# A graph kernel on one core: the edges' attention scores picked with one-hot products, in four parts, instead of gathered in two

## The reference

```python
h_proj = jnp.einsum('nd,rde->rne', h, relation_weight)
t_r = h_proj[etype, src]
h_r = h_proj[etype, dst]
att = jnp.sum(t_r * jnp.tanh(h_r + efeat), axis=-1)
seg_max = jax.lax.stop_gradient(jax.ops.segment_max(att, dst, num_segments=N))
att_exp = jnp.exp(att - seg_max[dst])
denom = jax.ops.segment_sum(att_exp, dst, num_segments=N)
a = att_exp / denom[dst]
h_nb = jax.ops.segment_sum(h[src] * a[:, None], dst, num_segments=N)
out = leaky_relu((h + h_nb) @ res_w1.T) + leaky_relu(h * h_nb @ res_w2.T)
```

## Time and profile before

| | us |
|---|---|
| median of three runs | 4488.78 |
| lowest and highest of them | 4483.08, 4492.01 |
| the profiled execution's own time | 4494.4 |
| its span | 4492.4 |
| busy: PE, DVE, ACT, POOL | 1605.1, 2361.7, 1340.0, 3099.8 |

### The profile page before, as it was taken

The page is one execution under the profiler, slowest core; times in us unless marked ns, Lnnn a source line. Parts: engine busy times, 40 slices in busy tenths (PEclk is TensorE's granted clock), DMA queues, the critical chain, the costliest instruction groups (busy, mean ns, idle before and its releaser), DMA issues.

```text
span 4492.4 us, 34467 instructions
## 1 busy us (share of the span) xinstructions
PE 1605.1 (36%) x8878; PEld 1252.6 (28%) x8878; DVE 2361.7 (53%) x3528; ACT 1340.0 (30%) x2772; POOL 3099.8 (69%) x3293
## 2 busy tenths in 40 slices
PE   6600088888566420000000000033356400466564
PEld 2200066666444210000000000022245300466553
DVE  9959877888899768887701111022222200444442
ACT  0012255656333211111110000122222100687773
POOL 8877787100388767777577777777747777487787
PEclk9955588999777655555555555555566555666665
DMA  2147777666344335555422222243433200122121
GB/s 52 40 131 247 239 225 235 219 211 225 117 123 120 95 111 196 175 200 186 170 58 73 74 73 74 89 127 124 129 95 92 82 1 0 35 58 62 56 57 28
DMA packets 362656, 528.19 MB, mean 118 GB/s; under 512 B 220064, under 2 KB 232458, under 8 KB 362470
## 3 DMA queue, kind: packets, MB, share of 16 engines
q1 hardware_dynamic: 268166, 426.25, 28.6%
q0 software_dynamic: 94304, 99.74, 9.5%
HBM read 265.55 MB, written 264.24 MB: 118 GB/s over the span
## 4 chain that ended last, share of the span: by engine, by line
POOL 53%; issue 18%; DVE 16%; PE 5%; DMA 4%; ACT 3%; SPq 1%; POOLq 0%; DVEq 0%; ACTq 0%
POOL arena L1202 21%; POOL result L1197 9%; POOL slot_rows L1197 8%; POOL relf L1202 8%; POOL work L1202 6%; DMA arena<-in_x 3%; DVE arena L522 1%; DVE arena L508 1%; POOL pause L1210 1%; DVE t_stat L513 1%; DVE t_stat L506 1%; PE banks L1611 1%; DVE arena L538 1%; DVE work L565 1%; DVE arena L561 1%
## 5 line engine op out<-in xcount | busy, mean ns | idle before, releaser
L1202 POOL DMA_INDIRECT arena<-input_and_place_by_node,src_i x252 | 313.2, 1243 | 461.0 <-DVE arena L641 386.5
L1197 POOL DMA_INDIRECT result<-work,outi x392 | 479.3, 1223 | 169.2 <-issue 122.1
L1202 POOL DMA_INDIRECT arena<-g_by_node_and_edge,m_idx x392 | 447.0, 1140 | 121.1 <-issue 119.2
L1202 POOL DMA_INDIRECT work<-in_x,dsafe x392 | 432.9, 1104 | 117.1 <-issue 62.3
L1197 POOL DMA_INDIRECT slot_rows<-work,dsafe x392 | 402.4, 1027 | 139.9 <-issue 119.2
L1202 POOL DMA_INDIRECT arena<-h_by_node_and_edge,m_idx x392 | 400.7, 1022 | 119.5 <-issue 119.2
L1202 POOL DMA_INDIRECT relf<-slot_scores,src_i x392 | 371.2, 947 | 150.1 <-issue 68.3
L1701 PE MATMUL banks<-ident,work 128*128 128x128 f32 x456 | 112.1, 395 | 874.3 <-DMA work<-slot_rows 873.2
L822 DVE TENSOR_TENSOR work<-work,ends 128x896 f32<-128x896 f32 x28 | 46.7, 1669 | 561.8 <-DMA work<-h_by_node_and_edge 556.5
L1701 PEld LDWEIGHTS banks<-ident,work 128*128 128x128 f32 x456 | 81.1, 204 | 890.2 <-issue 689.6
L565 DVE SCALAR_TENSOR_TENSOR work<-work 128x1024 f32<-128x1024 f32 (+1 forms) x77 | 116.6, 1514 | 298.3 <-ACT work L1520 238.9
(11 more groups left out here) (320 smaller groups left out, 5606.4 us busy)
## 6 DMA issues: line engine op xcount, KB each, us to landing
arena<-in_x SPq DMA_DIRECT2D x96, 512.0 KB, 5.2
slot_rows<-work SPq DMA_DIRECT2D x48, 912.0 KB, 8.7
work<-slot_rows SPq DMA_DIRECT2D x114, 384.0 KB, 3.3
input_and_place_by_node<-arena SPq DMA_DIRECT2D x49, 528.0 KB, 2.7
arena<-input_and_place_by_node SPq DMA_DIRECT2D x49, 512.0 KB
g_by_node_and_edge<-arena SPq DMA_DIRECT2D x49, 512.0 KB, 2.6
h_by_node_and_edge<-arena SPq DMA_DIRECT2D x49, 512.0 KB, 2.6
arena<-x_of_destination SPq DMA_DIRECT2D x56, 448.0 KB, 4.1
```

The costliest lines, as they stand in the source:

```text
L1197: pool.indirect_dma_start(out=table[:, :], out_offset=bass.IndirectOffsetOnAxis(ap=idx, axis=0), in_=of, in_offset=None, bounds_check=boun ...
L1202: pool.indirect_dma_start(out=to, out_offset=None, in_=table[:, :], in_offset=bass.IndirectOffsetOnAxis(ap=idx, axis=0)).then_inc(signal, 16)
```

## The change

Edges are split into four parts in the order in which they are sent: steps 0 to 7, 8 to 15, 16 to 23 and 24 to 27 of the permute stage, that is 112, 112, 112 and 56 columns. Each part has its own slots: 144, 144, 144 and 88 tiles, 520 in place of 456, so 130 quadruples in place of 114. Part 0 is counted in the first edge stage and placed in the second; parts 1 to 3 are counted and placed inside the permute stage (`sort_next`): 32 counts in step 0, 8 and 16, and 32 placements over the next five steps.

A score now stays in SBUF. An edge knows its tile and its lane. For a pair of columns TensorE spreads the edges' lanes over the partitions (`spread_lanes`), VectorE compares them with the partition's own number, which gives a one-hot matrix (`lanes_hot`), TensorE multiplies that with the part's scores, so that each edge's partition holds the scores of its lane in all tiles (`find_scores`), and VectorE picks the edge's tile with a compare, a multiply and a sum, one instruction a column (`scores_picked`). There are 196 pairs.

`spread_work` sets how many quadruples and pairs stand in each step, by a room of 35 a step, 3.0 a quadruple and 1.9 a pair. Its table, worked out from the code: steps 9, 10 and 11 have 11 quadruples of part 0 each, step 12 has 3 and 13 pairs, steps 13 and 14 have 18 pairs, step 15 has 7. Steps 17 to 23 repeat that with part 1. Steps 25, 26 and 27 have 11 quadruples of part 2 each. What is left stands after the last step: 3 quadruples and 56 pairs of part 2, then 22 quadruples and 28 pairs of part 3. The 392 gathers of scores and the two stores are gone. The four relation numbers come with one load. The slots' zeroing is 60 stores of 1664 columns in place of 48 of 1824.

```diff
-HALF = KE // 2
-KH = 228
-KS = 2 * KH
+PART_STEPS = (0, 8, 16, 24, 28)
...
+            runs, room = [[] for _ in range(GE + 1)], 0.0
+            left = [(k, kind, cost, n) for k in range(PARTS)
+                    for kind, cost, n in (("score", 3.0, PART_TILES[k] // RG), ("pick", 1.9, (PART_COLS[k][1] - PART_COLS[k][0]) // 2))]
...
+            def lanes_hot(i):
+
+                dve.wait_ge(pick["spread"], i + 1)
+                after(dve, pick["found"], i - 1)
+                ts(lane_hot[:, i % 2, :], bank(6)[:, 0:2 * P], lane_no[:, 0:1], None, ALU.is_equal).then_inc(pick["hot"], 1)
+
+            def scores_picked(k, i):
+
+                dve.wait_ge(pick["found"], i + 1)
+                n = PART_TILES[k]
+                for c in range(2):
+                    t = 2 * i_column(k, i) + c
+                    after(dve, pick["done"], 2 * i + c)
+                    stt(out=picked[:, 0:n], in0=tile_no[:, 0:n], scalar=tile_of[:, t:t + 1], in1=bank(7)[:, c * KH:c * KH + n],
+                        op0=ALU.is_equal, op1=ALU.mult, accum_out=att[:, t:t + 1]).then_inc(pick["done"], 1)
...
             step_c(0)
             for s in range(GE):
                 if s + 1 < GE:
                     step_c(s + 1)
-                rel_some(*first_part_span(s))
-            rel_some(NJ, 2 * NJ)
-
-
-            o = Steps(dve, soft)
-            dve.wait_ge(score_got, 16 * KE)
+                sort_next(s)
+                follow(s)
+            follow(GE)
+
+
+            o = oe
+            dve.wait_ge(pick["done"], KE)
...
-            pool.wait_ge(sort, at_step["score rows"])
-            for k, at in enumerate((range(HALF, KE), range(0, HALF))):
-                pool.wait_ge(scored, 16 * (k + 1))
-                for t in at:
-                    (gather if k else gather_slowly)(att[:, t:t + 1], att_t[k], score_row[:, t:t + 1], score_got)
...
-                number = [pe.value_load(tile_reli[0:1, j * RG + k:j * RG + k + 1], min_val=0, max_val=R - 1)
-                          for k in range(RG)]
+                pe.load(number_regs, tile_reli[0:1, j * RG:(j + 1) * RG])
+                number = [pe.snap(reg, min_val=0, max_val=R - 1) for reg in number_regs]
...
+            def spread_lanes(k, i):
+
+                n = PART_COLS[k][1] - PART_COLS[k][0]
+                after(pe, pick["hot"], i)
+                for c in range(2):
+                    at = 2 * (i - pair_of(k, 0)) + c
+                    ins = matmul(bank(6)[:, c * P:(c + 1) * P], ident[0:n, at:at + 1].to_broadcast([n, P]), lanes_t[0:n, :],
+                                 start=True, stop=True)
+                ins.then_inc(pick["spread"], 1)
+
+            def find_scores(k, i):
+                n = PART_TILES[k]
+                pe.wait_ge(pick["hot"], i + 1)
+                after(pe, pick["done"], 2 * i)
+                for c in range(2):
+                    ins = matmul(bank(7)[:, c * KH:c * KH + n], lane_hot[:, i % 2, c * P:(c + 1) * P], slot_score[k % 2][:, 0:n],
+                                 start=True, stop=True)
+                ins.then_inc(pick["found"], 1)
```

More of the change, by code:

```diff
@@ L66 @@
 SB = 3
-ZW = 1824
+ZW = 1664
 ZN = KS * RW // ZW
@@ L341, in build @@
         rel_in = ring("rel_loaded", SB)
-        scored, score_got = sem("scores_stored"), sem("scores_here")
-        soft = sem("softmax_steps")
-        f = sems("f", "steps mat weighed run share nb two masked summed turned t o os half out")
+        pick = sems("pick", "turned lanes spread hot found done")
+        edge_steps = sem("edge_steps")
+        f = sems("f", "mat weighed run share nb two masked summed turned t o os half out")
         f_in, f_sent = ring("f_loaded"), ring("f_sent")
@@ L591, in _ @@
             all_landed(dve, own_kept, OWN_KEPT)
-            oe = Steps(dve, S["steps"])
+            oe = Steps(dve, edge_steps)
             for q in range(2):
@@ L681, in _ @@
             os = Steps(dve, sort)
-            od = Steps(dve, G["steps"])
+            od = oe
             od.did(v.memset(zero, 0.0))
@@ new lines, in tile_relation, with place @@
+            def tile_relation(k, r):
+                n = PART_TILES[k]
+                os.do(stt(out=tile_rel[0:1, 0:n], in0=tile_no[0:1, 0:n], scalar=cnt[0:1, 2, r:r + 1],
+                          in1=tile_rel[0:1, 0:n], op0=ALU.is_ge, op1=ALU.add))
+            def place(k, r):
+                lo, hi = PART_COLS[k]
+                at, one, run = pos[:, 0:hi - lo], tmp_b[:, 0:hi - lo], tmp_b[:, P:P + hi - lo]
+                os.do(ts(one, relf[:, lo:hi], rel_no[:, r:r + 1], None, ALU.is_equal))
+                os.do(v.tensor_tensor_scan(out=run, data0=onesk[:, 0:hi - lo], data1=one, initial=cnt[:, 4, r:r + 1],
@@ L889, in _ @@
             at_step["exponents"] = o.n
-            of = Steps(dve, f["steps"])
+            of = oe
             of.did(v.memset(fmat.rearrange("p (f t) -> p f t", t=SC)[:, :, 0:1], 0.0))
@@ L1488, in rel_some, with follow @@
                     rel_tanh(j)
-            act.wait_ge(C["steps"], at_step["c mat"])
+            def follow(s):
+                for kind, k, lo, hi in work_at[s]:
+                    if kind == "score":
+                        rel_some(PART_TILE0[k] // RG + lo, PART_TILE0[k] // RG + hi)
+                    elif lo == 0:
+                        n = PART_COLS[k][1] - PART_COLS[k][0]
+                        act.wait_ge(pick["turned"], k + 1)
+                        copy(lanes_t[0:n, :], bank(6)[0:n, 0:P]).then_inc(pick["lanes"], 1)
+            act.wait_ge(edge_steps, at_step["c mat"])
             c_mat(0)
@@ L1714, in rel_project @@
                 ins.then_inc(rel["tr"], 1)
-            pe.wait_ge(sort, at_step["tiles"])
             pe.wait_ge(loaded, 16 * (N_LOADS + 2))
@@ new lines, in _ @@
+            for s in range(GE + 1):
+                if s < GE and s in PART_STEPS and step_part(s) + 1 < PARTS:
+                    relation_totals(step_part(s) + 1)
+                for kind, k, lo, hi in work_at[s]:
+                    if kind == "score":
+                        if lo == 0:
+                            pe.wait_ge(sort, at_step[f"tiles {k}"])
+                        rel_some(PART_TILE0[k] // RG + lo, PART_TILE0[k] // RG + hi)
+                    else:
+                        pick_some(k, lo, hi)
```

303 lines of the change are left out of this document (182 added, 121 removed).

## The result

The changed kernel took 4305.68 us, the median of four runs (4295.19 to 4327.24), beside 4486.83 for four runs of the kernel before (4483.08 to 4492.01). The ratio is 0.9604, 95% interval 0.9573 to 0.9635: 181 us faster, where 100 were forecast. The profiled execution of the changed kernel is the slowest of its four, so between the two traces the spans differ by 167.0 us (4492.4 to 4325.4).

A forecast was written before the change was run, and what follows sets the result against it. The prediction took GpSimd's DMAs, and the issue gaps between them, to bound the kernel. Softmax sooner (-99) and the port (-11, +10) sum to -100: 4494.4 to 4394, less 5.6 for the median, 4388 us; 8 in 10 range 4295 to 4480.

The forecast's parts named there:

- the forecast's own case: Whole kernel: 60 to 140 us gained, its own range 4350 to 4430 us, chance 0.52.
- the case of over 140 us: Whole kernel: more than 140 us gained, with faster loops or GpSimd never waiting; chance 0.2.
- Softmax at 3739: After the permute stage: the step-by-step sum starts the softmax at 3739, 99 us sooner than before.
- Quadruple 3.3: Score loop: 3.3 us a quadruple in place of 4.4, bounds 2.7 and 4.4; 429 us for all 130.
- rival of loops as slow as today's: Score loops: a quadruple stays near 4.4 us, adding 143 us to give 4531, slower; chance 0.1.
- Pair 2.1: Picking loop: 2.1 us a pair, 1.95 or 2.45 by clock level, bounds 1.8 and 2.6; 412 us for 196.
- rival of fast loops: Score loops: the clock rises and both run at their lower bounds, 137 us more gained, 4251; over 140 gained 0.2.
- GpSimd waits on ScalarE's copies: Permute stage: scatters of steps 11 to 16 and 19 to 24 wait 5 to 25 us each, the last 35 to 40.
- The port: GpSimd's gathers beside VectorE's two-source sort: 11 us gained in the second edge stage, 10 lost in the permute stage.
- The first edge stage: Counting has half the instructions there, but GpSimd's gathers set the end: nothing, at most 10 us gained.
- What comes ahead of it: Before 2230, ahead of the permute stage: nothing is touched but for the sort.
- Zeroing at nothing: Second edge stage: 6.3 MB more zeroing costs nothing at DMA share 0.55; 34 us if uncovered.

The follow-up runs named there:

- e1: The kernel before with one load of a quadruple's four relation numbers in place of four reads; 4471.01 us, ratio 0.9974.
- e2: The changed kernel with the four separate reads of relation numbers put back; 4479.12 us, ratio 0.9983 to the kernel before.
- e3: The changed kernel without spreading, comparing, finding and picking, so the edges' scores are not filled; 4105.46 us, ratio 0.9145.
- e4: The changed kernel with two PSUM banks each for the spread lanes and the found scores; 4234.79 us, ratio 0.9449.
- e5: The kernel before with 24 extra VectorE instructions in each of permute steps 2 to 13, four kinds; 4951.16 us beside 4964.87.
- e6: e8 with parts ending at steps 8, 15, 22 and 28 and a room of 38 where nothing is sorted; 4677.88 us, ratio 0.9411.
- e7: e4 with the last part's spreading product over 112 rows in place of 56; 4695.36 us, ratio 0.9442.
- e8: e4 with room 22 in sorting steps, 33 in others, and loops priced at 2.9 and 1.2; 4726.24 us, ratio 0.9505.
- e9: e4 again, word for word, in the third batch; ratio 0.9522 to the kernel before.
- e10: e7 again beside e9, the last part's spread over 112 rows; 40 us below e9 by the medians.

## Why the forecast was right, and by how much off

The bottleneck, the waits and where they fall came out as forecast. The size did not: 181 us is outside the forecast's own case, 60 to 140 us gained, which had 0.52. It is the case of over 140 us that came, which had 0.2, and the time is inside the range for 8 in 10, 11 us from its fast end. So that it was faster, and by which path, was foreseen; how much faster was not.

**Softmax at 3739.** It started at 3674.9, 64 us sooner, though the permute stage started 4.4 later.

**Quadruple 3.3.** It was 2.93. 130 x 0.37 = 48 us. The loop had been worked out as 3.0 and raised for a clock of about 0.7 and for transposes that are no longer covered. The row shows 0.80 behind the last scatter and 0.70 from 2620 to 2990. A quadruple is 2.9 to 3.0 us in the long runs of the first and 3.0 to 3.2 in those of the second, so the raise was too large at either. That the reads were what held it is shown by e1 and e2: 4.4 to 3.2 and 2.93 to 3.97. The rival of loops as slow as today's is out for this kernel. With four loads in place of one, e2, the time is the same as before within 0.2%.

**Pair 2.1.** It was 1.69 at the upper level where 1.95 was forecast, 2.23 at the lower for 2.45, and 1.81 in the mean, for a lower bound of 1.8. 196 x 0.29 = 57 us. The term that was mis-sized at the upper level is the find: 0.9 and a semaphore of 0.1 were priced, and from its start to the first pick it is 0.77. The two picks came close to their price, 0.76 for 0.84, and the way back to TensorE was 0.16 for 0.1. At the lower level the loop itself was another: spread was said to lie beside the picks, and there find and spread follow one another on TensorE without a gap, 1.08 and 1.15 us, and the picks lie beside them. The clock was the reason that the rival of fast loops gave, and it is the smaller part of this: 168 pairs at the forecast's 1.95 and 28 at its 2.45 make 2.02 in the mean.

**From 105 us to 64.** Quadruples and pairs together make 105 us on paper. From a part's first load to its last pair, part 0 took 295 us where 330 was forecast (2649.0 to 2943.7), part 1 281 for 310 (2994.1 to 3275.2), and parts 2 and 3 to the softmax 350 for 390: 104 us. Of these, 6 were lost because part 0 started later than forecast, and 34 between the parts, where 50 and 49 us passed without a quadruple or a pair, in place of 27 and 39. In SyncE's queue the first load of part 1's tiles stands behind `load_features(19)`, which waits until the scatters of step 17 have landed. The last of these started at 2989.1, the features' loads were issued from 2991.4 on, and the tiles' first load at 2994.1, where 3000 was forecast. So of the 30 us saved ahead of it 6 were left. Part 1's own scatters end with step 15, and the last of those started at 2912.3. So the load waited for its place in the queue and not for its data, and ahead of part 2 it was the same (3243.8 and 3324.6); what another order would gain no run tried.

**GpSimd waits on ScalarE's copies.** Found where named: the scatters of steps 12 to 15 and 20 to 23 came 42 to 52 us after those of the step before, in place of 37.3, and the last ones 48. The wait was 89.8 us, and 30 more of "issue" than the 119.2 before, against over 120. So the last scatter started at 3386.0 for 3414 (less 11), and 289 us came back behind it for about 320. Steps 11, 16, 19 and 24, which were also named, didn't wait.

**The port.** -11 and +10 were priced, at 0.16 us for each us of VectorE. Both sizes were wrong and nearly cancelled in the sum. The first six steps of the permute stage, which hold the sort of part 1 and no score work, are the clean case. Before, then after:

```profile
2287.70:2509.80 222.10, 0.00 (x0) 0.00 (x0) 23.34 (x18) 20.86 (x18) 170.89 (x169) 0.50 0.25 74
```

```profile
2292.10:2516.50 224.40, 0.00 (x0) 0.00 (x0) 81.46 (x195) 20.91 (x18) 173.22 (x169) 0.50 0.27 73
```

58 us of sort, most of it with two sources in SBUF, cost GpSimd 2.3 us and not 9. The second edge stage, from its first gather to its last, took 561.8 us for 564.3: 2.5 gained, and 4.7 to 5.8 in e2, e3 and e4, not 11. The rule of the Trainium skill (GPSIMD Engine Reference, 8. Key points), that GpSimd contends with VectorE instructions with two SBUF inputs, is borne out by the earlier trace rows, where the VectorE instruction is 1.68 us long and the gather beside it 2.34, by all 218 gathers named under e5, and by the scatters of e5 of 1.35 us beside an instruction of 0.57. What failed is the step that made one price for each busy us out of rows with long instructions. A hold is the rest of one instruction, less about 0.15 us, and a long instruction is hit more often as well, so by this reckoning its price goes with the square of its length. An estimate from these numbers, with one DMA every 1.33 us: the sort's 159 instructions of 0.27 to 0.45 us cost 2.9 us in the six steps, and 2.3 were measured.

**The first edge stage.** At most 10 us were allowed for, and taken as nothing. It gained them: 408.3 us from its first gather to its last before, 398.5 after, 397.1 to 397.2 in e2 to e4 and 409.6 in e1, which is the kernel before in this. The mean gather went from 1321 to 1282 ns. The counts themselves held nothing: of the kernel before's gathers the 27 that lie beside a count more than beside anything else take 943 ns, like those beside nothing. What changed is which gathers fall on the long two-source instructions. Over what an undisturbed one takes, the gathers beside the product ahead of the scan (L641, L677 after) lose 19 us before and 5 after, and those beside the scan 30 and 35. So these 10 us come from how the two engines' instructions fall together, which nothing in the forecast foresaw.

**What comes ahead of it.** The forecast said that nothing before 2230 is touched but for the sort. Yet the first edge stage's first gather starts at 1211.1 us in place of 1191.7, at 1194.6 to 1208.4 in e2 to e4, and at 1180.2 in e1. In the second batch it is 1349 to 1365 in e6, e7 and e8, and 1316 in e5. So this gather comes later in every changed kernel than in any kernel before of its batch, by 3 to 31 us in the first and 33 to 49 in the second. The sum put this term at nothing. Between the two main traces it is 19 us, more than the two gains above, and the permute stage starts 4.4 us later. Its cause was not looked into.

**Zeroing at nothing.** Right: the stage that holds it, the second edge stage, got no longer.

What stays open: the node layers, 23 us of e2, the 4 us by which the stretch behind the softmax's start is shorter in every changed kernel of the first batch, the 100 us between the parts, and whether even room or other parts would pay in the first batch, where GpSimd waited only 30.1 us in the kernel with two banks, and 387.0 in the third.

## What to carry to other kernels

Write down a chain of engines that wait for one another as a loop with a period, at both clock levels, and multiply by its count; then ask for each term whether it lies in the serial run, since the same edit was worth 15 us outside it and 173 inside. When the long pole is taken out (392 gathers here), the next bound is the work that takes its place, and it is worth a second buffer at once: 71 us here. And a wait of the engine that used to be the pace is no cost of its own once another chain sets the end: 66 us more of it changed nothing. Check at both clock levels which engine closes the loop: here it was find and picks at the upper one, and TensorE alone at the lower.

## What the runs showed of the hardware

- Four registers come with one load for nearly the price of one, 0.33 us (L1799) for 0.30 (L1706): with it a quadruple's period falls by 1.0 us in the kernel after and by 1.2 in the kernel before.
- A gather of GpSimd that starts inside a VectorE instruction with two sources in SBUF ends 0.70 to 0.83 us after it, in 218 of 218 cases of the kernel before, whether it is 0.36 or 2.16 us long. A gather that starts inside a reduction is not held (43 cases), nor in e5 one that starts inside an instruction with a source in PSUM (21 cases).
- The same busy share of TensorE goes with either level of the clock. The last 28 pairs of e9 ran at 0.50 with TensorE busy 58.00 of 58.00 us, the 56 pairs ahead of them at 1.00 with it busy 59.45 of 60, and the last 28 of e10, whose spread had 112 rows in place of 56, at 0.90. With 84 rows (e6) it was 0.99. How the two depend on each other was not looked into further.
- The same kernel took 4486 us in one batch and 4965 and 4961 in two others, and the cause is open. In e9 the first three quadruples of steps 10, 11, 18 and 19 come 8 to 18 us apart, and 2 to 6 in e4, the same kernel in the first batch; GpSimd waits 387.0 us for 30.1. It is not the loads of slots alone: pairs, which load nothing, come up to 15 us apart in step 14 and 17 in step 22 of e9, and at most 1.8 in e4. Behind the last scatter both kernels' pairs take the same 1.1 us. The kernel with two banks kept its gain, 0.9449 and 0.9522, but not its size.
